# Second gate and candidate banks, and four output-product banks, for the late tiles of the second FFN

## What is computed

```python
def ffn(x):                      # scan over axis 0: 8 steps of a 1024 x 256 state
    c = broadcast(in_c)
    for xt in x:
        ft = sigmoid(xt @ wf.T + c @ uf.T + bf)
        it = sigmoid(xt @ wi.T + c @ ui.T + bi)
        gt = tanh(xt @ wc.T + c @ uc.T + bc)
        c = ft * c + it * gt
    return tanh(einsum('tbi,oi->tbo', x, wo) + c @ uo.T + bo)
x = x + 0.5 * ffn(layernorm(x))
x = x + attention(layernorm(x))  # gated delta rule, a scan over 1024 tokens
x = x + 0.5 * ffn(layernorm(x))
```

## Time and profile before

| what | value |
|---|---|
| time, median of 3 runs | 1365.33 us (1364.75, 1365.33, 1370.57) |
| time of the profiled execution | 1362.08 us |
| its span | 1360.3 us |
| TensorE busy | 1261.8 us (93%) |
| TensorE's granted clock, mean over the span | 0.98 |
| VectorE, ScalarE, GpSimd busy | 63%, 49%, 20% |

### The profile page before, as it was taken

The page is one execution under the profiler, slowest core; times in us unless marked ns, Lnnn a source line. Parts: engine busy times, 40 slices in busy tenths (PEclk is TensorE's granted clock), DMA queues, the critical chain, the costliest instruction groups (busy, mean ns, idle before and its releaser), DMA issues.

```text
span 1360.3 us, 57987 instructions
## 1 busy us (share of the span) xinstructions
PE 1261.8 (93%) x25763; PEld 1167.5 (86%) x25763; DVE 856.1 (63%) x2047; ACT 665.3 (49%) x1623; POOL 273.3 (20%) x350
## 2 busy tenths in 40 slices
PE   6999999999999999898898889899999999999997
PEld 6989998989989888787778887888889989898886
DVE  4556886868778676567657764854445646354622
ACT  3344444454444545453564556356455756655432
POOL 0113112031221211112502230230230405050500
PEclk9999999999999999998899999899999999999999
DMA  4010101122121222242225213323324242333000
GB/s 147 1 63 32 66 33 67 65 79 65 52 80 51 103 70 90 69 129 71 69 65 166 66 54 112 109 83 108 117 91 147 66 134 82 110 102 109 1 32 31
DMA packets 72425, 108.35 MB, mean 80 GB/s; under 512 B 12400, under 2 KB 49520, under 8 KB 70128
## 3 DMA queue, kind: packets, MB, share of 16 engines
q1 hardware_dynamic: 72176, 104.65, 24.0%
HBM read 53.74 MB, written 50.86 MB: 77 GB/s over the span
## 4 chain that ended last, share of the span: by engine, by line
PE 75%; DVE 12%; ACT 7%; issue 5%; DMA 0%; SPq 0%; DVEq 0%; ACTq 0%
PE ps L471 41%; PE ps L543 7%; PE ps L899 6%; PE ps L1093 5%; PE ps L1110 4%; PE ps L706 3%; ACT gates L488 3%; ACT zbd L1127 2%; PE ps L431 2%; DVE ln_bn L83 2%; PE ps L735 1%; DVE hs L557 1%; PE ps L870 1%; PE ps L696 1%; DVE ffn_rows L568 1%
## 5 line engine op out<-in xcount | busy, mean ns | idle before, releaser
L471 PE MATMUL ps<-gates,wt 128*128 128x128 f32 x2688 | 350.5, 283 | 2.9 <-DVE gates L517 2.9
L471 PEld LDWEIGHTS ps<-gates,wt 128*128 128x128 f32 x2688 | 320.9, 195 | 14.0 <-DVE gates L517 3.6
L471 PE MATMUL ps<-ffn_rows,wt 128*128 128x128 f32 x2304 | 296.7, 281 | 10.1 <-DVE hs L557 3.7
L471 PEld LDWEIGHTS ps<-ffn_rows,wt 128*128 128x128 f32 x2304 | 276.6, 195 | 20.1 <-issue 12.5
L488 ACT ACTIVATE gates<-ps,colv 128x128 f32<-128x128 f32 x448 | 127.6, 369 | 194.8 <-PE ps L471 194.5
L515 DVE TENSOR_TENSOR fcig<-gates 128x512 f32<-128x512 f32 x112 | 83.9, 750 | 163.5 <-ACT gates L495 129.8
L1134 DVE TENSOR_TENSOR zbd<-ps,mask 64x1024 f32<-64x1024 f32 x63 | 76.5, 1214 | 127.9 <-PE ps L1110 127.9
L1196 POOL TENSOR_TENSOR ffn_rows<-ffn_rows,rowv 128x256 f32<-128x256 f32 x64 | 53.9, 878 | 347.0 <-DMA ffn_rows<-x_scratch 347.0
L1127 ACT ACTIVATE zbd<-ps,mask 32x256 f32<-32x256 f32 x252 | 103.8, 458 | 9.9 <-PE ps L1110 6.9
L899 PE MATMUL ps<-inv_cols,kv 32*32 32x32 f32 x8192 | 88.3, 194 | 15.8 <-issue 13.7
L899 PEld LDWEIGHTS ps<-inv_cols,kv 32*32 32x32 f32 x8192 | 79.1, 104 | 27.7 <-issue 18.7
(11 more groups left out here) (127 smaller groups left out, 1726.8 us busy)
## 6 DMA issues: line engine op xcount, KB each, us to landing
xs_scratch<-xs_out SPq DMA_DIRECT2D x32, 512.0 KB, 3.5
xsb<-xs_scratch SPq DMA_DIRECT2D x256, 64.0 KB
ffn_rows<-x SPq DMA_DIRECT2D x32, 256.0 KB, 3.4
x_scratch<-ffn_rows SPq DMA_DIRECT2D x32, 256.0 KB, 2.7
kg_scratch<-kg_rows SPq DMA_DIRECT2D x32, 256.0 KB, 2.8
kgb<-kg_scratch SPq DMA_DIRECT2D x256, 32.0 KB, 2.3
e_scratch<-e SPq DMA_DIRECT2D x256, 32.0 KB, 1.7
ffn_rows<-e_scratch SPq DMA_DIRECT2D x8, 1024.0 KB
```

The costliest lines, as they stand in the source:

```text
L471: mm = pe.matmul(banks[g][:, col:col + P], wt[:, w, k, m * P:(m + 1) * P], rhs, start=(x in (0, FI)), stop=(k == KT - 1 and (t == 0 or x > ...
```

## The change

From tile 3 of the second FFN on (`WIDE` = 3), banks 6 and 7 serve as second gate bank and second candidate bank, alternating with banks 0 and 1 by the parity of the step. The output products of tiles 3 to 6 take four banks (0, 1, 6, 7), so none waits for another to be read; the first step of tiles 4 to 7 waits for products 0 and 1 alone (`freed` 3), the second step for all four. In the last tile the gates alternate (0 and 6), the candidate keeps bank 1 alone, and the output products go to banks 4, 5, 3 and 7, with waits for the hops' last use of bank 3 and for VectorE's read of the tile before from bank 7. The first step that uses banks 6 and 7 (tile 3, step 1) waits for their last read by the preparation. No arithmetic, no transfer and no order of instructions is changed.

```diff
--- before.py
+++ after.py
@@ -176,6 +176,7 @@
 SECOND = TILE * NB
 AT_POST = TILE
 END = SECOND + TILE * NB + 3
+WIDE = 3
 
 
 def hop_at(i):
@@ -405,22 +406,31 @@
                 self.h_read, self.h_act, self.x_done = sem(f"{tag}_h_read"), sem(f"{tag}_h_act"), sem(f"{tag}_x_done")
 
 
-            def fi_b(self, b):
-                return [ps[0], ps[1]] if b.n < self.solo else [ps[0]]
-
-            def g_b(self, b):
-                return [ps[2], ps[3]] if b.n < self.solo else [ps[1]]
+            def wide(self, b):
+                return self.fr == "fr2" and b.n >= WIDE
 
             def last(self, b):
                 return self.fr == "fr2" and b.n == NB - 1
 
+            def fi_b(self, b):
+                if self.wide(b):
+                    return [ps[0], ps[6]]
+                return [ps[0], ps[1]] if b.n < self.solo else [ps[0]]
+
+            def g_b(self, b):
+                if self.wide(b) and not self.last(b):
+                    return [ps[1], ps[7]]
+                return [ps[2], ps[3]] if b.n < self.solo else [ps[1]]
+
             def h_b(self, b):
                 if self.last(b):
-                    return ps[4:8]
+                    return [ps[4], ps[5], ps[3], ps[7]]
+                if self.wide(b):
+                    return [ps[0], ps[1], ps[6], ps[7]]
                 return [ps[0], ps[2], ps[1], ps[3]] if b.n < self.solo else [ps[0], ps[1], ps[0], ps[1]]
 
             def freed(self, b, t):
-                return (3, 5)[t] if b.n < self.solo else 5
+                return (3, 5)[t] if b.n < self.solo or (b.n > WIDE and self.wide(b)) else 5
 
             def pe_front(self, pe, b, fills):
                 for j in fills:
@@ -449,7 +459,7 @@
             def pe_step(self, pe, b, t, lo=0, hi=2 * NX):
                 fi_b, g_b = self.fi_b(b), self.g_b(b)
                 turns = len(fi_b)
-                banks = (fi_b[t % turns], g_b[t % turns])
+                banks = (fi_b[t % turns], g_b[t % len(g_b)])
                 full = (self.fi_full, self.g_full)
                 for x in range(lo, hi):
                     if t == 0 and x >= NX:
@@ -461,10 +471,13 @@
                             emptied(pe, self.fr, b.n, t // 2 + 1)
                         if t < turns:
                             wait_pos(pe, self.h_read, 5 * (b.n - 1) + self.freed(b, t))
+                            if t == 1 and self.wide(b) and b.n == WIDE:
+                                for at in (6, 7):
+                                    pe.wait_ge(bank[at].read, LAST_READ[at])
                         else:
                             pe.wait_ge(self.fi_read, 8 * b.n + t - turns + 1)
                     if x == FI and t > 0:
-                        wait_pos(pe, self.g_read, 8 * b.n + t - turns + 1)
+                        wait_pos(pe, self.g_read, 8 * b.n + t - len(g_b) + 1)
                     if x == NX:
                         pe.wait_ge(self.c_done, 8 * b.n + t)
                     rhs = self.xnT[b.n % len(self.xnT)][:, k, t, :] if x < NX else cst[t % 2][:, k * P:(k + 1) * P]
@@ -529,9 +542,13 @@
             def pe_h(self, pe, b, j, halves=(0, 1)):
                 h_b = self.h_b(b)
                 if self.last(b):
-                    if 0 in halves:
+                    if 0 in halves and j < 2:
                         pe.wait_ge(bank[4 + j].read, LAST_READ[4 + j])
                         pe.wait_ge(z_done, STATE_OPS * (HOPS - 1))
+                    elif 0 in halves and j == 2:
+                        pe.wait_ge(e_done, HOPS)
+                    elif 0 in halves:
+                        pe.wait_ge(self.h_read, 5 * b.n)
                 elif j == 0 and 0 in halves:
                     pe.wait_ge(self.fi_read, 8 * b.n + 8)
                 if 0 in halves and h_b[j] is self.g_b(b)[-1]:
```

More of the change, by code:

```diff
@@ L405, in __init__, with last @@
                 self.h_read, self.h_act, self.x_done = sem(f"{tag}_h_read"), sem(f"{tag}_h_act"), sem(f"{tag}_x_done")
+            def wide(self, b):
+                return self.fr == "fr2" and b.n >= WIDE
+            def last(self, b):
+                return self.fr == "fr2" and b.n == NB - 1
             def fi_b(self, b):
+                if self.wide(b):
+                    return [ps[0], ps[6]]
                 return [ps[0], ps[1]] if b.n < self.solo else [ps[0]]
             def g_b(self, b):
+                if self.wide(b) and not self.last(b):
+                    return [ps[1], ps[7]]
                 return [ps[2], ps[3]] if b.n < self.solo else [ps[1]]
-            def last(self, b):
-                return self.fr == "fr2" and b.n == NB - 1
             def h_b(self, b):
                 if self.last(b):
-                    return ps[4:8]
+                    return [ps[4], ps[5], ps[3], ps[7]]
+                if self.wide(b):
+                    return [ps[0], ps[1], ps[6], ps[7]]
                 return [ps[0], ps[2], ps[1], ps[3]] if b.n < self.solo else [ps[0], ps[1], ps[0], ps[1]]
             def freed(self, b, t):
-                return (3, 5)[t] if b.n < self.solo else 5
+                return (3, 5)[t] if b.n < self.solo or (b.n > WIDE and self.wide(b)) else 5
             def pe_front(self, pe, b, fills):
```

## The result

| | before | after |
|---|---|---|
| median | 1365.04 us (1357.97 to 1370.57, 4 runs) | 1344.56 us (1340.15 to 1349.15, 4 runs) |
| profiled execution, span | 1362.08, 1360.3 us | 1342.28, 1340.5 us |
| ratio | | 0.9863, 95% interval 0.9824 to 0.9901 |

The change makes the kernel faster, by 20.5 us between the medians and 19.8 between the two spans. Measured again, the same kernel came to 1350.13 against 1364.09 (ratio 0.989, 0.9857 to 0.9923), which is 14 to 15 us, and 1350.13 lies inside the range. So there are two questions: what the changed part gives, and what else is in the 20.

What follows compares the result with a forecast made beforehand. TensorE was taken to bound the kernel, with gains only at tile boundaries and after the hops: 5.9 + 0.5 + 2.29 + 2.5 = 11.2 us, so 1365.3 - 11.2 = 1354.1 us, range 1348.5 to 1361.

Steps and rivals of the forecast that it cites:

- The two waits that were to grow: Tile 6's fourth step, for VectorE's state, 0.34 to about 1.2 us; ahead of tile 7's transposes, 0.51 to about 1.7.
- Rival A: Tile 6: every stop goes, five more steps at 0.40 us; 13.1 us in all, 1352.2 us; chance 0.13.
- B: Tiles 6 and 7: the state's loop replaces the banks as limit; 8.3 us gain left, 1357.0 us; chance 0.09.
- C: Boundaries beside hops give their gain back; 4.8 us less, 6.4 in all, 1358.9 us; chance 0.09.
- D: Change does not act, because another wait in the same place ends as late; 1365.3 us; chance 0.04.
- Rival E: Tiles 6 and 7: denser bank alternation lowers TensorE's clock to 0.79, costing 28 us, 1382 us; chance 0.03.
- the size of a block without a stop: Blocks of 24 rows take 2.78 us; tile 6's step becomes 5.56 us, tile 7's 6.42.
- 1.13 and 2.29 us: Waits for VectorE's reads of output products that go: 1.13 at boundaries beside hops, 2.29 into tile 7.
- the tanh stop: Boundaries into tiles 3, 4 and 5: the second input part's wait for the tanh goes, 0.83 us each.
- no idle time to lose inside tiles 3 to 5: Inside tiles 3 to 5 nothing is gained or lost.
- the cost with two ends: Tiles 3 to 5: VectorE operations slowed by GpSimd; from 0.38 us gained to 7 us lost, taken as no change.
- the 0.1 of tile 6: Tile 6, before the transposes: shorter steps move VectorE's start 0.2 us behind GpSimd's end, gaining 0.1 us.

Runs made afterwards that it cites:

- the run with GpSimd helped: Changed kernel, with VectorE multiplying and adding three of GpSimd's eight rows in tile 6; 1342.63 us, ratio 0.9826.
- the last two experiments: Changed kernel with second banks from tile 4, then with a single candidate bank; tile 3's first slot to the end took 336.17 and 335.86 us.
- output banks alone: Changed kernel with gates and candidate back to one bank each, four output banks kept for tiles 3 to 6; ratio 0.9935 to the kernel before.

## Why the prediction was wrong, point by point

**The places were right.** Every stop that the prediction said would go is gone, and where it said that nothing would move, little has, but for tiles 3 and 5 (below): nothing inside tile 4 (58.84 us in both), nothing from tile 6's second state part to the transposes (37.91 against 37.90, where the sum had 0.1), nothing behind the last state part. The two waits that were to grow grew to 1.59 and 1.53 (about 1.2 and 1.7 forecast). Rival A, that tile 6 gives all its stops, is out, and the run with GpSimd helped shows whose path it is. Rivals B, C and D are out by the table. Rival E is out: the granted clock of the changed kernel is 1.00 (2.4 GHz) over all tiles with second banks (busy time, one stretch):

```profile
1014.00:1330.00 316.00, 311.26 (x5115) 294.81 (x5115) 165.74 (x385) 172.75 (x461) 73.35 (x96) 1.00 0.28 85
```

So the warning of the Trainium skill about cycling through PSUM banks ("TensorE: Matmul & The Clock Gate", "A second HAM failure mode: psum-queue depth-cycling") does not apply to this rhythm: TensorE was not left idle between groups, it is busy 311.26 of 316 us here.

**The step that failed first is the size of a block without a stop.** I took 2.78 us for 24 rows, from a block that stands between hops. That block ends at the hop's first products, matmuls of another shape. In tiles 6 and 7 state parts and input parts follow each other in one shape, and there a block takes 2.68 us (1236.43 - 1233.75). The trace of before held this figure, in the first FFN, whose banks alternate from the start (TensorE, kernel before):

```profile
32.91 2.84 PE L471 MATMUL ps<-gates,wt 128*128 128x128 f32 x24
35.59 2.84 PE L471 MATMUL ps<-ffn_rows,wt 128*128 128x128 f32 x24
38.27 2.84 PE L471 MATMUL ps<-gates,wt 128*128 128x128 f32 x24
```

That is the changed tile's step, 5.36 us, measured before the change was made; I used this stretch for the clock alone and not for the length. Two blocks of 0.10 in each of tile 7's six steps are 1.2 us, the same in tile 6's first step 0.2, and the blocks of the first slots of tiles 6 and 7 some 0.4.

**The same error at the boundaries.** There I added the idle times of the timeline, 1.13 and 2.29 us. A stop costs more than its idle column. In tile 6 one can see where the rest lies: a block's row reads 2.84 us while without a stop the next block starts 2.68 after it, so the column hides 0.16; and the block behind a stop takes 2.79 (1252.28 - 1249.49) and not 2.68. That makes 0.34 + 0.16 + 0.11 = 0.61, and the step shrank by 0.60 (5.96 to 5.36). So too the last tile: the earlier trace rows leave it 2.4 us of idle time, and its six steps alone gave 3.68. At the boundaries the distances between starts shrank by 1.4 (into tiles 4 to 6, output banks alone) and 2.8 us. I had seen this at the tanh stop (0.83 by distance, 0.46 by the column; 0.72 to 0.76 measured), yet went by the column at the others: 0.3 us too little at three boundaries and 0.5 at the fourth, 1.4 us.

**A term that was missing.** The stop of 0.9 to 1.2 us in tile 3's second slot stood in the timeline of before (1031.91) and the prediction has no term for it: that TensorE has no idle time to lose inside tiles 3 to 5 was read from tile 4 alone. It goes with the wait for the tanh, as the last two experiments foretold and showed, and is worth 1.2 us (the slot takes 9.21 us before and 7.99 after). The wait alone does not make it: in the kernel before, the boundaries into tiles 4 and 5 have the same wait of 0.46 and no such stop behind it. In the transfer records of the trace the two 16 KB instruction fetches nearest to the place start 17.3 and 20.7 us after slot 88's hop in the kernel before and 12.8 and 18.9 in the changed one; the eight other profiles divide in the same way, by whether they have the stop. That TensorE's instruction stream, held at the tanh, is fetched too late for the next block is argued from these times, not shown.

In tile 5 0.4 us went the other way, by the cost with two ends that the prediction had named and taken as no change. Eight of the twelve small VectorE operations now fall under GpSimd's additions there, where none did before, and TensorE waits 0.53 us for the state (changed kernel):

```profile
1193.76 0.65 DVE L95 SCALAR_TENSOR_TENSOR ln_stats<-ln_bn,ln_stats 128x8 f32<-128x8 f32 x1
```

```profile
1197.34 2.05 PE L484 MATMUL ps<-gates,wt 128*128 128x128 f32 x16 [0.53 <-DVE gates L530]
```

(In tile 3 of the kernel before it is seven that are slowed, not the eight of the prediction.) These terms together, 1.2 + 0.2 + 0.4 + 1.4 + 1.2 - 0.4, are 4.0 us against the 3.5 that were missing; the tanh stops, forecast 0.1 too high at each of three boundaries, and the 0.1 of tile 6 account for the rest.

**The range failed by what lies ahead.** 14.7 us less than 1365.33 is 1350.6, inside the range. The other 5.1 us between the two first profiles come from the part ahead of slot 88, which varies by 15.7 us over the profiles of this study with nothing changed in it; that the rest between the medians (20.5 less 14.7) comes from there too is argued, since only one execution of each run has a trace. I had three times of before with 5.8 us between them and a profiled run 3.3 below their median, and allowed 3.5 us for this at the lower end. The range was made of the change's own unknowns and left out most of the kernel's. (Its lower end was rounded too: A less 3.5 us is 1348.7, not 1348.5, which makes no difference here.) The 3.5 us that the sum missed would alone have stayed inside, and the repeated run did stay inside; the 5.8 us from outside the change would alone have led to 1354.1 - 5.8 = 1348.3, just below the lower end. So the step that took the time out of the range is the 3.5 us allowed for the untouched part, where the profiles have 15.7 between their ends.

## What to carry to other kernels

When an edit brings one stage the rhythm of another, read the length of a step in that other stage, in the same trace, before adding up idle columns: a stop costs the distance between two starts less the distance without the stop, in the same sequence of shapes. Count stops only as far as the next engine on the path allows; in tile 6 five of six were worth nothing because GpSimd and VectorE set the end. And where an untouched stretch varies from run to run, compare the changed stretch in the traces, and give the range of the whole time the width of the rest.

## What the runs showed of the hardware that was not expected

TensorE stopped for 0.9 to 1.2 us after 53 or 54 of a hop's 64 second products, in tile 3's second slot of each of the five profiles in which it waits for the tanh a slot earlier, and of none of the five in which it doesn't. One scaling of 128x1024 elements on VectorE took 1.75 to 1.77 us in the six profiles in which GpSimd's first addition had started before it (by 0.04 to 0.85 us), and 1.22 in the four others. And with the same instructions the 526 us of hops and preparation were run at a mean granted clock of 0.94 to 0.98, which goes with 15.7 us of the time, as large as the whole effect of the change.
